# A two-layer decoder on one core: a batch's first projections one step earlier in causal attention, and the experts' next rows transposed ahead of the inner values

## The reference, cut to what matters

```python
q = jnp.einsum('bsd,qd->bsq', x, wq).reshape(B, S, H, D).transpose(0, 2, 1, 3)
kv_latent = jnp.einsum('bsd,ld->bsl', x, w_kv_down)
k = jnp.einsum('bsl,ql->bsq', kv_latent, w_k_up).reshape(B, S, H, D).transpose(0, 2, 1, 3)
...
q = q * cos + _rotate_half(q) * sin
k = k * cos + _rotate_half(k) * sin
scores = jnp.einsum('bhsd,bhtd->bhst', q, k) / jnp.sqrt(jnp.float32(D))
causal = jnp.triu(jnp.full((S, S), -jnp.inf, dtype=jnp.float32), k=1)
scores = scores + causal[None, None]
```

```python
h = jax.nn.silu(jnp.einsum('btd,edf->betf', xn, W1))
y = jnp.einsum('betf,efd->betd', h, W2)
out = jnp.einsum('bte,betd->btd', wdense, y)
```

## Time and profile before

| | |
|---|---|
| median of 3 runs | 4176.59 us (4171.93 to 4178.02) |
| profiled execution, its own time | 4185.04 us |
| its span, first to last instruction | 4183.2 us |
| mean granted TensorE clock | 0.912 of full |
| PE busy | 3380.4 us, 81% of the span |
| DVE, ACT, POOL busy | 51%, 47%, 22% |
| causal attention (`a1`) | about 1370 to 2417 us of the span |
| experts, 72 tiles | about 3421 to 4060 us of the span |

### The profile page before, as it was taken

The page is one execution under the profiler, slowest core; times in us unless marked ns, Lnnn a source line. Parts: engine busy times, 40 slices in busy tenths (PEclk is TensorE's granted clock), DMA queues, the critical chain, the costliest instruction groups (busy, mean ns, idle before and its releaser), DMA issues. The chain is left out here.

```text
span 4183.2 us, 72856 instructions
## 1 busy us (share of the span) xinstructions
PE 3380.4 (81%) x25752; PEld 2491.4 (60%) x25752; DVE 2143.3 (51%) x6691; ACT 1949.6 (47%) x4754; POOL 935.2 (22%) x724
## 2 busy tenths in 40 slices
PE   6888888767697788888898879999996429999970
PEld 3565565567586466666665657777775316666650
DVE  4777777679676445555545534555544301111116
ACT  5778777633421555655556536566653101111110
POOL 0000000034000766666766400000000440000014
PEclk9999999978798899999999989999998569999995
DMA  2000000010201222221221110000002520001113
GB/s 74 12 12 18 12 12 8 12 46 16 94 1 45 56 55 58 57 54 46 60 57 49 40 43 25 20 17 17 22 12 87 193 75 31 30 29 31 31 38 107
DMA packets 120192, 178.06 MB, mean 43 GB/s; under 512 B 23776, under 2 KB 75424, under 8 KB 119328
## 3 DMA queue, kind: packets, MB, share of 16 engines
q1 hardware_dynamic: 113696, 156.61, 12.7%
q0 software_dynamic: 6144, 16.79, 1.3%
HBM read 90.88 MB, written 32.11 MB: 29 GB/s over the span
## 5 line engine op out<-in xcount | busy, mean ns | idle before, releaser
L893 ACT ACTIVATE a_t<-a_t,a_neg 128x512 f32<-128x512 f32 (+3 forms) x1024 | 643.0, 634 | 9.4 <-DVE a_neg L1070 7.9
L720 PE MATMUL a_T<-ident,a_t 128*128 128x128 f32 x3328 | 503.8, 286 | 76.7 <-ACT a_pT L884 58.7
L884 ACT ACTIVATE a_pT<-a_T 128x512 f32<-128x512 f32 (+3 forms) x896 | 415.9, 502 | 309.9 <-PE a_T L720 308.9
L720 PEld LDWEIGHTS a_T<-ident,a_t 128*128 128x128 f32 x3328 | 381.1, 145 | 267.5 <-issue 234.7
L1065 DVE CUSTOM_DVE_ANT_0 a_t<-a_A,a_table 128x384 f32<-128x384 f32 (+3 forms) x512 | 221.4, 487 | 343.9 <-PE a_A L697 341.7
L1065 DVE CUSTOM_DVE_ANT_0 a_t<-a_A,a_decay 128x512 f32<-128x512 f32 x512 | 323.0, 687 | 98.9 <-PE a_A L685 98.7
L2076 PE MATMUL experts_H<-ex_w,experts_xgT 128*128 x576 | 268.9, 610 | 40.3 <-ACT experts_xgT L2103 40.3
L2126 DVE COPY experts_y<-experts_Y 128x256 f32<-128x256 f32 x72 | 30.6, 425 | 511.4 <-PE experts_Y L2064 511.4
L921 POOL TENSOR_TENSOR a_rsin<-a_rawswapped,a_sin 128x512 f32<-128x512 f32 x128 | 166.7, 1302 | 558.2 <-DMA a_rawswapped<-a_raw 544.4
L1065 DVE CUSTOM_DVE_ANT_0 x_t<-x_A,x_table,x_mx 128x512 f32<-128x512 f32 x256 | 177.0, 748 | 169.2 <-PE x_A L697 169.0
L2064 PE MATMUL experts_Y<-ex_w,experts_hT 128*128 x1152 | 260.5, 379 | 1.0 <-DVE experts_hT L2135 1.0
(11 more groups left out here) (277 smaller groups left out, 7022.2 us busy)
## 6 DMA issues: line engine op xcount, KB each, us to landing
a_rawswapped<-a_raw SPq DMA_DIRECT2D x512, 64.0 KB, 2.0
a_invrep<-a_inv_dram SPq DMA_DIRECT2D x64, 256.0 KB, 3.9
ex_w<-in_f_w_dram SPq DMA_DIRECT2D x16, 1024.0 KB, 13.6
moe_sent<-route_zeros SPq DMA_DIRECT2D x1, 9216.0 KB, 29.9
experts_xg<-moe_sent SPq DMA_DIRECT2D x72, 128.0 KB, 2.2
moe_results<-experts_y SPq DMA_DIRECT2D x72, 128.0 KB, 1.7
a_xin<-x_all SPq DMA_DIRECT2D x16, 512.0 KB, 3.0
x_xin<-x_all SPq DMA_DIRECT2D x16, 512.0 KB, 4.1
```

Source lines behind the costliest of these rows:

```text
L720: mm = pe.transpose(bank[:, kt, :], t_of(u, j, kt * P, (kt + 1) * P), sh.ident[:])
L884: nc.scalar.activation(to, of, ACT.Copy).then_inc(t_empty, 1)
L893: nc.scalar.activation(t_of(u_e % U, j, 0, n), t_of(u_e % U, j, 0, n), ACT.Exp, bias=neg[:, slot, j:j + 1], scale=SCALE, accum_out=total[: ...
```

## The change

In `a1` the items of the next batch's group 0 move one step ahead: items 0 and 1 from step 13 to step 12 (behind `lat`), items 2 and 3 from step 14 to step 13. So that four pieces of work fit in step 12, they stand at the places 1, 2, 3 and 4, which also moves `lat` from place 3 to place 2. In the experts, `X` of the next tile moves from behind `HT` to ahead of it. Nothing is added or removed.

```diff
@@ tasks, for the items of the next batch's group 0
-            items = {"a0": ([], [0], [1], []), "a1": ([], [0, 1], [2, 3], []), "x1": ([], [0, 1], [2, 3], [4])}[kind]
+            items = {"a0": ([], [0], [1], []), "a1": ([0, 1], [2, 3], [], []), "x1": ([], [0, 1], [2, 3], [4])}[kind]
...
-        found += [(1 + 2 * k if len(works) > 1 else 1, work) for k, work in enumerate(works)]
+        found += [(1 + k * (1 if len(works) > 2 else 2), work) for k, work in enumerate(works)]
@@ experts, PE's step
                 if not first:
                     down(i - 1, 1 - parity)
+                if more:
+
+                    transpose_rows(1 - parity, pair + (parity + 1))
                 for half in range(2):
                     pe.wait_ge(h_act, i * 2 + (half + 1 + 2))
                     for j in range(FT // 2):
                         f = half * (FT // 2) + j
                         mm = pe.transpose(HT[half][:, j, :], h[:, f * P:(f + 1) * P], sh.ident[:])
                     mm.then_inc(ht_full, 1)
-                if more:
-
-                    transpose_rows(1 - parity, pair + (parity + 1))
```

## The result

| | before | after |
|---|---|---|
| median | 4177.31 us (4171.93 to 4180.18, 4 runs) | 4121.06 us (4116.68 to 4124.21, 4 runs) |
| profiled span | 4183.2 us | 4120.2 us |
| mean granted clock | 0.912 | 0.913 |

The ratio is 0.9866 (95% interval 0.9849 to 0.9883): 56 us less. The range held the time, at its upper edge, but the likeliest case did not come: the experts gave their part, and causal attention gave no gain that can be measured.

A forecast was written before the change was run, and what follows sets the result against it. PE was taken to set the time in experts and attention, through its idle time and lower clock. 57 us (experts) plus 34 us (attention) make 91 us, so 4176.6 becomes 4086 us; range 4068 to 4122 us.

The forecast's parts named there:

- the likeliest case: Whole kernel: both parts gain as worked out, 4086 us likeliest, 4073 to 4120 us with other sizes; chance 0.76.
- Forecast 57 us: Experts: `HT` hides ACT's copy and the first weights load beside it, 0.80 us in each of 71 tiles.
- The register read: Experts: reading the expert's number (0.305 us) stays hidden behind `HT`; the rival that it is exposed, 4143 us, had chance 0.05.
- attention gives nothing: Rival, attention: POOL's wait becomes an equal wait for step 15's maxima, SP holding the inverted sums; 4120 us, chance 0.11.
- DVE needs 5 us of delay to cancel the gain, and the same pattern shows 2: Batch transitions in attention: the argument against attention giving nothing, comparing the DVE delay needed with the first batch's pattern.
- Forecast 2.1 us earlier: Attention, last transition: POOL starts the next batch's group 0 at 2243.0 instead of 2245.16.
- `a_oT`, undersized: Attention, step 15: `a_oT` comes 15.9 us behind POOL's start, 2.1 us later than before the change.
- The clock, with the wrong sign: Behind each batch transition: shorter waits bring back 1.8 of the 2.9 us lost at the 0.50 clock.
- The sum of 34 us: Attention: 3.1 us gained on arrival plus 1.8 us of clock, together 4.9 us in each of seven transitions.
- nothing, if DVE's chain comes later than I work out: Attention: the lower bound on the gain; the upper bound was 42 us.
- DVE shut out by POOL: Rival, attention: DVE loses 1.1 us at `a_rsum` and at a negation per transition, 15 us off the gain; 4101 us, chance 0.05.
- Slower by clock: Rival, experts: PE without pause gets less clock; a third of tiles, 32 of 71, would cancel 91 us; chance 0.03.

The follow-up runs named there:

- e6: Kernel after with the experts' transposes `X` between the two halves of `HT` instead of ahead of both; 0.9920 of the time before, experts 593.6 us.
- e3: Kernel after with SP issuing the swap of the next batch's item 3 one step later, behind the inverted sums; 0.9777 of the time before, 4085.98 us.
- e4: Kernel after with three buffers for the swapped halves instead of two, and one semaphore less in routing; 0.9773 of the time before, 4085.0 us.
- e8: Kernel after with three swap buffers and the load of the next input rows three steps later; 0.9791 of the time before, attention 1042.7 us.
- e2: Kernel after with the experts' transposes back in the old order, so only the attention change stays; 0.9993 of the time before.
- e7: Kernel after with the load of attention's next input rows issued three steps later, still two swap buffers; 0.9860 of the time before.
- e9: Kernel after with three swap buffers, but SP's wait for POOL put back at item 3 of every group; 0.9840 of the time before.
- e10: Kernel after with three swap buffers and SP's wait at item 3 put back in groups 1 to 3 only; 0.9806 of the time before.

## Why the prediction was right and where it was wrong

**Experts, right.** Forecast 57 us, measured about 58. The copy is done ahead of the end of `HT`, the weights are loaded beside the last transposes, 0.98 us behind the start of `X` (the chain was 0.94 before), and e6 shows what half the cover costs. The register read stayed hidden.

**Attention, wrong.** The sum was 91 us and 56 came; the range held only because it was drawn to take in the rival "attention gives nothing", put at 0.11. Its mechanism was named rightly: the wait for POOL becomes one for the maxima of step 15, since SP holds the inverted sums back. Only the "wait of equal length" was not so: it was half as long, and the clock did the rest. The failing step is the argument against this rival, "DVE needs 5 us of delay to cancel the gain, and the same pattern shows 2". Piece by piece, from the scores of step 11:
- *POOL, right.* Forecast 2.1 us earlier; measured +12.9 against +15.2, 2.3 us, in transitions 2 to 6. In the last it was 1.7 us, since the swap took 4.67 us from SP's issue to POOL, not 4.02. POOL's 22.4 us for the group were as forecast.
- *`a_oT`, undersized.* It came 16.05 us behind POOL's start in the last transition, as forecast (15.9), but 16.4 to 17.2 us in the others. So it was 2.4 to 3.5 us later than before, 3.0 in the mean, not 2.1.
- *The clock, with the wrong sign.* I took it as a gain of 1.8 us behind the transition. It is also a price: the new wait, half as long as the old, pulled it down in six of seven places and cost 0.9 to 1.8 us at once, 1.3 in the mean. Delay and price together are 4.3 us of the 5, and the gain on arrival is 1.0 us in the mean, not 3.1.
- *What follows, left out.* I stopped at the first scores of the new batch. At the next scores of the last transition PE was 3.7 us ahead of before, against 4.9 in the sum; at L660 a longer wait (1.6 us) and its clock (1.55 us) took nearly all of that back. I had not looked for the next place where PE needs DVE.

The signs came as this says: no wait for POOL at the seven places, but a wait of `a_oT` for `a_invrep` of 4.5 to 5.6 us where 1 to 3 were expected, and a clock of 0.56 behind the last transition's wait, not above 0.7.

**The sum of 34 us** would have been nearly right without the hold: 36 to 40 us measured in e3, e4 and e8. There the first scores of a batch come at about +35.4 (transitions 2 to 6), 3.3 us earlier than before, where 3.1 were forecast; the rest is the clock. The bound "nothing, if DVE's chain comes later than I work out" was the outcome, and deserved more than a bound.

**DVE shut out by POOL** did show, though not where it cost the time. The mean does not move: `a_rsum` took 909 ns in the mean of 124 before and after. But its place does. Before, two `a_rsum` of 1.28 us together stood ahead of L1002 and two of 2.36 us behind it; after, the two of 2.36 us stand right ahead of it in all seven transitions, and L1002 starts 1.4 us behind the end of L757 (2.0 in the last), where it followed at once. These rows (1.28 us with POOL idle, 2.36 beside its work) agree with the Trainium skill's rule ("SBUF — State Buffer", "Who interferes with whom") that a DVE instruction with two SBUF inputs and a GpSimd instruction that reads SBUF exclude one another. In the kernel after, SP's hold outlasts this delay; in e3 and e4 the sums leave as soon as they are ready, but there the first scores wait for POOL anyway. **Slower by clock** did not come: the clock was 1.00 with PE busy all the time, and the tile's period is 7.98 us (from `Y` to `Y`), as forecast. (32 of 71 tiles are 45%, not the third that I wrote there.)

## What to carry to other kernels

An engine's queue that issues DMAs for several consumers is an engine like any other: when a step moves up, read which waits its DMAs carry and who stands behind them in that queue. Here a wait of about 1.4 us there, seven times, stood between nothing and a gain of 36 us: moving one issue behind the urgent one, or one more buffer, set it free, and the wait put back took 27 us again. When comparing two traces, take as origin the last work that the change cannot touch; an origin ahead of a place where the clock varies puts its accidents into the difference. Taken from the L757 that stands 10 to 11 us ahead of the scores of step 11, the last transition after would look 0.85 us slower than it is, all of it from products behind a wait that both kernels have. When a wait is traded for a shorter one, price the clock behind the new wait too, and follow the engine to its next two meeting points with others before you book the gain. A change that measures as nothing may be half of a pair: neither the placing nor the buffer gave anything alone.

## What was not expected of the hardware

A wait of 2.28 us was followed by nearly as low a clock (0.56 over 3.4 us) as one of 5.38 us (0.50 over 5.8 us). In six of the seven transitions after, the four products behind waits of 2.28 to 3.20 us took 2.91 to 3.78 us; in one, behind 3.09 us, 1.98. Behind waits of 0.64 to 1.63 us in e3 and e4 they took 1.98 in all fourteen. Between 2.1 and 3.9 us it is not certain: of the 35 such waits at this place in after, e2, e6, e7 and e9, seven (of 2.21 to 3.09 us) left the clock up, 28 did not.

Stages whose instructions no experiment touches differed between profiles. The start of causal attention lay at 1349.8 us in e4 and at 1371.1 us in e10, two kernels that differ in one constant of a later stage. From 900 to 1200 us (columns as above), e4, then e10:

```profile
900.00:1200.00 300.00, 233.77 (x1453) 210.18 (x1453) 236.97 (x530) 109.65 (x182) 67.27 (x44) 0.86 0.11 42
```

```profile
900.00:1200.00 300.00, 232.52 (x1398) 209.42 (x1398) 236.82 (x523) 110.42 (x183) 77.31 (x51) 0.82 0.11 42
```

The granted clock is 0.86 in one and 0.82 in the other. Whether this goes with the kernel or with the execution stays open; it is why parts are compared here by the length of their own stage.
